# Graph and expert layers on one core: another order of VectorE's and TensorE's steps in the first node stage

## The chip, the core and the metric

The kernel runs on one core of a Trainium2 chip. A core has five engines that run their own instruction streams in order and wait for each other through semaphores: TensorE (PE, with its weight loads PEld), VectorE (DVE), ScalarE (ACT), GpSimd (POOL) and SyncE (SP), which issues most DMAs. The metric is the device time of one execution in microseconds (us), the median of the runs.

## The reference

Four layers follow each other on x, 10000 rows of 512 floats: a graph attention layer (8 heads of 64), an expert layer (8 experts, the best one of each row), a graph convolution and a second expert layer. The change is in the stage that ends the first layer and does the whole of the second for every row:

```
out = segment_sum(w[:, :, None] * x_l[src], dst)      # attention: own row and listed edges
x = x + elu(out + bias) + layernorm(x)
router_logits = xf @ Wr + br                          # xf = layernorm(x)
h  = relu(xf @ W1[e] + b1[e])                         # e = argmax(router_logits)
oe = h @ W2[e] + b2[e]
x = x + gate * oe                                     # one expert: the gate is 1
```

The stage also prepares the rows that the graph convolution gathers: the layernorm of the new x, scaled by a number a row.

## The kernel before

The rows lie in 79 tiles of 128 (NT = 79). The kernel is a row of stages with a barrier between two. The first node stage stands in lines 954 to 1385 of the profiled program; in it each engine goes through its own list of steps with `tiles_in_turn(NT, steps)`:

```
for t in range(n + max(lag for lag, _ in steps)):
    for lag, step in steps:
        if 0 <= t - lag < n:
            step(t - lag)
```

So in turn i of an engine a step with lag k works on tile i - k, and within a turn the steps run in the order in which the list names them. Nothing else orders the work of an engine; it can't pass a step whose semaphore is not there. The turns of different engines are tied by these semaphores alone. This is what is done for a tile, with the lag before, the tile written and the line:

- POOL: `edge_rows` gathers the tile's edge sums (ai, L1050); `average` (lag 3) adds ta and ts into oc (L1059); `minus_mean1` and `root1` make the numbers of the layernorm for two tiles at once (L1066, L1073, L1076).
- DVE: `listed_part` and `self_part` (lag 2) multiply edge sums and own row by their shares (ta L1183, ts L1190); `positive` (4) makes xq from oc and the residual (L1199); `negative` (5) makes x1 and its sum (L1211); `hidden` (11) takes the 264 columns of the up product out of PSUM, times the root, plus bias (hb, L1218); `best`, `its_number`, `number_f`, `one_hot` (11) find the expert (L1224 to L1241); `routed` (11) keeps the hidden values of that expert (hm, L1247); `add_experts` (14) adds the down product out of PSUM to x1 and gives x2 (L1260). Small steps once in four tiles (L1134 to L1167: softmax shares; L1268 to L1279: slopes and shifts) stand between.
- PE: `turn1` (8) transposes x1 (4 transposes, L154), `up` (9) multiplies it by wc (L148), `turn_h` (12) transposes hm (3 transposes, L154), `down` (13) multiplies by w2 and b2p (L1317, L1319).
- ACT: `exp_of` (4, mi, L1341), `spread1` (8, sum of squares, L1356), once in four tiles `exp_group` (L1331), `copy_h` (12) takes the transposed hidden values out of PSUM (hT and hTb, L1364 and L1365), `spread2` (19, L1373), `copy1` (8) takes the transposed x1 out of PSUM (x1T, L1347), `scaled` (25, gs, L1380).
- SP loads (L1026, L1029) and stores (L1033, L1037).

The waits that tie the turns of PE, ACT and DVE: `up(t)` waits for `copy1(t)` (c_x1T) and, since PSUM has two buffers, for `hidden(t - 2)` (c_hb); `copy1(t)` waits for `turn1(t)`; `copy_h(t)` waits for `turn_h(t)`; `down(t)` waits for `copy_h(t)` and `add_experts(t - 2)`; `turn_h(t)` waits for `routed(t)`; `add_experts(t)` waits for `down(t)` and `scaled(t - 12)`.

## Time and profile before

| | |
|---|---|
| median of 3 runs | 2910.95 us (2907.52 to 2920.2) |
| the profiled execution | 2923.28 us, its span 2921.6 us |
| first node stage | about 1069 to 1517 us of the span |
| PE, DVE, ACT, POOL busy over the whole span | 76%, 63%, 32%, 61% |
| granted TensorE clock, mean | 0.89 |

Busy time is the sum of an engine's instructions. The records of DVE and ACT overlap a little: the next one starts some 0.07 to 0.12 us before the last has ended, so what a step costs its engine is the distance from its start to the next one's start. A DVE record also grows when the instruction has to wait while it is on the engine, so a busy DVE may be a waiting one.

### The profile page before, as it was taken

The numbers are of one execution on the slowest core, as the hardware profiler recorded it, in microseconds if no ns is written. First come the engines' busy times: TensorE is split into PE (matmuls) and PEld (weight loads), VectorE is DVE, ScalarE is ACT, GpSimd is POOL, SyncE is SP. The second block draws the span as 40 slices with busy tenths as digits, with TensorE's granted clock in tenths as the row PEclk, the third lists the DMA queues.
The fourth block names the chain that finished last, engine by engine and source line by source line (L and its number), as shares of the span: only waits on it lengthen the run. The fifth ranks groups of instructions, "written<-read, shape, count | busy, mean of one in ns | idle before, by whom it ended". The sixth has DMA issues, their size and how long they took to land. (4 is left out here: it accounts for less than half of the span.)

```text
span 2921.6 us, 43538 instructions
## 1 busy us (share of the span) xinstructions
PE 2216.3 (76%) x11528; PEld 1300.0 (44%) x11554; DVE 1838.4 (63%) x5166; ACT 920.5 (32%) x2016; POOL 1786.6 (61%) x2143
## 2 busy tenths in 40 slices
PE   8999999847776737999978759999995677773000
PEld 3444444325554525666644326666663444442000
DVE  4776677524444449999941116777776567676666
ACT  1111111025444514777763315555553000000000
POOL 4555555566666437888736635777776555553776
PEclk9999999959999968999989979999997799997555
DMA  6655555467888746788749966667762899995999
GB/s 202 221 191 187 180 187 191 148 182 243 261 253 250 221 135 195 245 265 260 240 167 347 354 217 211 213 217 216 217 202 71 263 356 351 346 308 191 349 369 342
DMA packets 361396, 698.57 MB, mean 239 GB/s; under 512 B 51609, under 2 KB 85235, under 8 KB 361153
## 3 DMA queue, kind: packets, MB, share of 16 engines
q1 hardware_dynamic: 239672, 399.69, 40.1%
q0 software_dynamic: 76720, 217.93, 24.4%
q10 hardware_dynamic: 44761, 78.17, 7.4%
q8 instruction: 96, 1.57, 0.2%
q14 instruction: 147, 1.20, 0.1%
HBM read 426.08 MB, written 287.17 MB: 244 GB/s over the span
## 5 line engine op out<-in xcount | busy, mean ns | idle before, releaser
L2069 POOL DMA_INDIRECT xg<-n_rows,ids x219 | 219.0, 1000 | 168.3 <-PE psum L154 97.7
L148 PE MATMUL psum<-wl,xT 128*128 128x512 f32 x632 | 288.8, 600 | 0.0
L148 PE MATMUL psum<-wg,yT 128*128 128x512 f32 x632 | 286.1, 596 | 0.0
L148 PE MATMUL psum<-wr,xT 128*128 128x512 f32 x632 | 284.1, 592 | 0.0
L2219 POOL DMA_INDIRECT q<-slot_outputs,qs x158 | 173.9, 1101 | 86.2 <-issue 47.8
L337 ACT ACTIVATE xb<-xa,xsc 128x512 f32<-128x512 f32 x79 | 64.2, 814 | 480.4 <-POOL xsc L397 480.4
L1654 POOL DMA_INDIRECT slot_tokens<-sl x158 | 167.2, 1058 | 70.3 <-issue 65.6
L2157 DVE COPY gT<-psum 128x512 f32<-128x512 f32 x219 | 142.0, 685 | 107.8 <-PE psum L154 82.4
L154 PE MATMUL psum<-ident,xg 128*128 128x128 f32 x876 | 154.1, 307 | 71.6 <-issue 40.7
L384 POOL TENSOR_TENSOR ve<-mv,epst 128x1 f32<-128x1 f32 x79 | 51.1, 647 | 254.4 <-DVE mv L439 254.4
L684 POOL DMA_INDIRECT gl<-xl_rows,idx x118 | 129.3, 1096 | 117.6 <-DVE vv L736 68.2
L148 PEld LDWEIGHTS psum<-wr,xT 128*128 128x128 f32 x632 | 120.1, 190 | 151.2 <-issue 151.2
L148 PE MATMUL psum<-wc,x1T 128*128 128x264 f32 x632 | 162.1, 400 | 32.7 <-DVE hb L1218 25.1
L154 PEld LDWEIGHTS psum<-ident,xg 128*128 128x128 f32 x876 | 107.9, 155 | 157.6 <-issue 146.2
L1059 POOL TENSOR_TENSOR oc<-ta,ts 128x512 f32<-128x512 f32 x79 | 138.6, 1755 | 57.8 <-DVE ta L1183 28.8
L148 PEld LDWEIGHTS psum<-wl,xT 128*128 128x128 f32 x632 | 115.0, 190 | 120.2 <-issue 120.2
L148 PEld LDWEIGHTS psum<-wg,yT 128*128 128x128 f32 x632 | 114.7, 192 | 114.4 <-issue 114.4
L533 DVE SCALAR_TENSOR_TENSOR xl<-psum,rs,gb_b 128x512 f32<-128x512 f32 x79 | 59.2, 750 | 163.8 <-PE psum L148 163.8
L736 DVE TENSOR_TENSOR vv<-gl,wt 128x512 f32<-128x512 f32 x118 | 80.2, 682 | 122.8 <-issue 82.5
L1414 POOL DMA_INDIRECT gg<-gcn_rows,idx x118 | 118.2, 1002 | 62.3 <-issue 30.9
L688 POOL DMA_INDIRECT gr<-xr_rows,idx x118 | 126.6, 1073 | 42.1 <-issue 34.7
L148 PE MATMUL psum<-hp,x3T 128*128 128x256 f32 x632 | 149.9, 380 | 2.5 <-ACT x3T L2007 2.5
(316 smaller groups left out, 5453.6 us busy)
## 6 DMA issues: line engine op xcount, KB each, us to landing
slot_outputs<-yo ACTq DMA_DIRECT2D x54, 1024.0 KB
x_rows<-x SPq DMA_DIRECT2D x158, 256.0 KB
edge_sums<-eo SPq DMA_DIRECT2D x29, 1056.0 KB
edge_sums<-go SPq DMA_DIRECT2D x29, 1024.0 KB
xT<-in_xTt SPq DMA_DIRECT2D x79, 256.0 KB
xl_rows<-xl SPq DMA_DIRECT2D x79, 256.0 KB
xr_rows<-xr SPq DMA_DIRECT2D x79, 256.0 KB
residual_rows<-xb SPq DMA_DIRECT2D x79, 256.0 KB
```

The lines of the kernel that those rows point to most:

```text
L148: last = nc.tensor.matmul(ps, lhs[:, k, :], rhs[:, k, :], start=(k == 0), stop=(k == DK - 1))
L154: last = nc.tensor.transpose(ps[:, k * P:(k + 1) * P], rows[:, k * P:(k + 1) * P], ident[:])
L337: act.activation(xb[:, s, :], xa[:, s, :], ACT.Identity, scale=xsc[:, s, 1:2], bias=xsc[:, s, 0:1]).then_inc(a_xb, 1)
L684: pool.indirect_dma_start(gl[:, w % 16, :], None, XL, bass.IndirectOffsetOnAxis(idx[:, 0, w:w + 1], 0), bounds_check=NP - 1, oob_is_err=Fa ...
L688: pool.indirect_dma_start(gr[:, w % 8, :], None, XR, bass.IndirectOffsetOnAxis(idx[:, 1, w:w + 1], 0), bounds_check=NP - 1, oob_is_err=Fal ...
L736: nc.vector.tensor_tensor(heads(vv[:, w % 8, :], CE)[:, :, 0:C], heads(gl[:, w % 16, :]), wt[:, u % 2, j, :].unsqueeze(2).to_broadcast([P, ...
L1059: pool.tensor_tensor(oc[:, t % 3, :], ta[:, t % 3, :], ts[:, t % 3, :], ALU.add).then_inc(c_o, 1)
L1414: pool.indirect_dma_start(gg[:, w % 8, :], None, GR, bass.IndirectOffsetOnAxis(idx[:, 0, w:w + 1], 0), bounds_check=NP - 1, oob_is_err=Fal ...
L1654: pool.indirect_dma_start(IDXF, bass.IndirectOffsetOnAxis(sl3[:, k, t:t + 1], 0), sl3[:, 2, t:t + 1], None, bounds_check=ME * SLOTS * P - ...
L2069: pool.indirect_dma_start(xg[:, t % 8, :], None, XN3, bass.IndirectOffsetOnAxis(ids[:, t:t + 1], 0), bounds_check=NP - 1, oob_is_err=False ...
L2157: nc.vector.tensor_copy(gT[:, t % 8, :, :].rearrange("p k n -> p (k n)"), bank[t % 2]).then_inc(p_T, 1)
L2219: pool.indirect_dma_start(q0[:, b % 3, t % 4, k, :], None, YL, bass.IndirectOffsetOnAxis(qs[:, b % 3, t % 4, k:k + 1], 0), bounds_check=LI ...
```

## The change

Only the lists of steps are changed, none of the steps. POOL's `average` goes from lag 3 to 2, `minus_mean1` from 6 to 5. On DVE `listed_part` and `self_part` come first, then `hidden` and `add_experts`; `positive` (lag 4 to 3), `negative` (5 to 4) and `routed` come last; the steps on slopes and shifts go from lag 21 to 22. On PE `up` and `down` stand together and the two groups of transposes behind them. ACT's `exp_of` and `spread1` go one lag down.

```diff
-                tiles_in_turn(NT, ((3, average), (9, pairwise(root1)), (6, pairwise(minus_mean1)), (15, fourwise(minus_mean2)),
+                tiles_in_turn(NT, ((2, average), (9, pairwise(root1)), (5, pairwise(minus_mean1)), (15, fourwise(minus_mean2)),
...
-                    (11, hidden), (5, negative), (0, once(larger, 0)), (21, fourwise(slopes)), (11, best), (2, listed_part),
...
+                    (2, listed_part), (2, self_part), (11, hidden), (0, once(larger, 0)), (14, add_experts), (11, best),
...
-                tiles_in_turn(NT, ((8, turn1), (9, up), (12, turn_h), (13, down)))
+                tiles_in_turn(NT, ((9, up), (13, down), (8, turn1), (12, turn_h)))
...
-                tiles_in_turn(NT, ((4, exp_of), (8, spread1), (0, exp_group), (12, copy_h), (19, spread2), (8, copy1),
+                tiles_in_turn(NT, ((3, exp_of), (7, spread1), (0, exp_group), (12, copy_h), (19, spread2), (8, copy1),
```

One turn of PE in the middle of the stage, and the first step of the next, before:

```order
L148 MATMUL psum<-wc,x1T 128x264 x4
L154 MATMUL psum<-ident,hm 128x128 x3
L1317 MATMUL psum<-w,hT 128x512 x2
L1319 MATMUL psum<-b2p,hTb 128x512
L154 MATMUL psum<-ident,x 128x128 x4
L148 MATMUL psum<-wc,x1T 128x264 x4
```

The same in the changed program (line numbers are one less there):

```order
L148 MATMUL psum<-wc,x1T 128x264 x4
L1316 MATMUL psum<-w,hT 128x512 x2
L1318 MATMUL psum<-b2p,hTb 128x512
L154 MATMUL psum<-ident,x 128x128 x4
L154 MATMUL psum<-ident,hm 128x128 x3
L148 MATMUL psum<-wc,x1T 128x264 x4
```

The transposes of hm (`turn_h`) have moved from behind `up` to the end of the turn; between them and the next `up`, where the down products and the transposes of x1 stood, nothing is left.

ACT's stream of the changed program at the same place, from the copy that waits for `turn_h` on:

```order
L1363 ACTIVATE hT<-psum 128x256
L1364 ACTIVATE hTb<-psum 128x128
L1372 ACTIVATE sq,sB<-x2,sB 128x512
L1346 ACTIVATE x1T<-psum 128x512
L1379 ACTIVATE gs<-x2,sB 128x512
L1340 ACTIVATE mi<-oc 128x512
```

It is what it was: `copy_h`, `spread2`, `copy1`, `scaled`, `exp_of`; only the tiles of `exp_of` and `spread1` are later ones by one.

One turn of DVE without the small steps, before, from `hidden` on:

```order
L1218 SCALAR_TENSOR_TENSOR hb<-psum,sA,b1b 128x264
L1211 SCALAR_TENSOR_TENSOR x1,sA<-mi,xq 128x512
L1224 MAX m8<-hb 128x8
L1183 TENSOR_TENSOR ta<-ai,fe 128x512
L1229 MAX_INDEX i8<-m8,hb 128x8
L1190 TENSOR_TENSOR ts<-li,fe 128x512
L1234 CAST ix<-i8 128x1
L1199 SCALAR_TENSOR_TENSOR xq<-oc,xx 128x512
L1241 TENSOR_TENSOR hm<-iota3,ix 128x128
L1260 SCALAR_TENSOR_TENSOR x2,sB<-psum,x1 128x512
L1247 SCALAR_TENSOR_TENSOR hm<-hb,hm 128x256
```

And now, from `add_experts` on to the next `hidden`:

```order
L1260 SCALAR_TENSOR_TENSOR x2,sB<-psum,x1 128x512
L1224 MAX m8<-hb 128x8
L1229 MAX_INDEX i8<-m8,hb 128x8
L1234 CAST ix<-i8 128x1
L1241 TENSOR_TENSOR hm<-iota3,ix 128x128
L1199 SCALAR_TENSOR_TENSOR xq<-oc,xx 128x512
L1211 SCALAR_TENSOR_TENSOR x1,sA<-mi,xq 128x512
L1247 SCALAR_TENSOR_TENSOR hm<-hb,hm 128x256
L1183 TENSOR_TENSOR ta<-ai,fe 128x512
L1190 TENSOR_TENSOR ts<-li,fe 128x512
L1218 SCALAR_TENSOR_TENSOR hb<-psum,sA,b1b 128x264
```

The two products that POOL's sum waits for now stand directly ahead of the two steps that read PSUM, and `routed` (hm<-hb,hm) stands as far from the start of that sum as it can.

## Rows read from the trace of the kernel before

**Rows 1.** The page: its engines' busy time, and DVE in 40 slices.
```profile
PE 2216.3 (76%) x11528; PEld 1300.0 (44%) x11554; DVE 1838.4 (63%) x5166; ACT 920.5 (32%) x2016; POOL 1786.6 (61%) x2143
...
DVE  4776677524444449999941116777776567676666
```

**Rows 2.** Busy time by stretch: PE, PEld, DVE, ACT, POOL, clock, DMA share, GB/s.
```profile
1150.00:1425.00 275.00, 257.73 (x1082) 168.89 (x1098) 274.90 (x902) 197.72 (x497) 224.66 (x230) 1.00 0.80 253
```

**Rows 3.** Groups of DVE, 1150 to 1425: count, busy us, mean ns, idle before.
```profile
L1247 DVE SCALAR_TENSOR_TENSOR hm<-hb,hm 128x256 f32<-128x256 f32 x55 | 48.2, 877 | 0.0
...
L1162 DVE RECIPROCAL rd<-rd 128x32 f32<-128x32 f32 x13 | 4.4, 342 | 0.0
```

**Rows 4.** Instructions on the tile hb, whole trace: min/median/max ns.
```profile
L1247 DVE SCALAR_TENSOR_TENSOR hm<-hb,hm x79: 413/883/1374, 1118.3 to 1499.9; 128x256 f32<-128x256 f32 x79
```

**Rows 5.** Timeline of POOL and DVE: start, duration, engine, line, tiles.
```profile
1311.87 1.72 POOL L1059 TENSOR_TENSOR oc<-ta,ts 128x512 f32<-128x512 f32 x1
...
1312.37 0.68 DVE L1260 SCALAR_TENSOR_TENSOR x<-psum,x 128x512 f32<-128x512 f32 x1
...
1312.98 0.88 DVE L1247 SCALAR_TENSOR_TENSOR hm<-hb,hm 128x256 f32<-128x256 f32 x1
```

**Rows 6.** Waits, 1100 to 1500: who waited for whom, us, times, longest.
```profile
ACT hT L1364 <- PE psum L154: 92.6, 70, 2.8
...
PE psum L148 <- DVE hb L1218: 25.1, 49, 2.9
```

**Rows 7.** Timeline of PE: the start of a turn, and the next turn.
```profile
1309.71 2.02 PE L148 MATMUL psum<-wc,x1T 128*128 128x264 f32 x8 [0.33 <-DVE hb L1218]
...
1314.41 2.02 PE L148 MATMUL psum<-wc,x1T 128*128 128x264 f32 x8
1316.27 0.49 PE L154 MATMUL psum<-ident,hm 128*128 128x128 f32 x3
1316.60 1.88 PE L1317 MATMUL psum<-w,hT 128*128 128x512 f32 x4
1318.32 0.38 PE L1319 MATMUL psum<-b2p,hTb 128*128 128x512 bf16 x1
1318.53 0.60 PE L154 MATMUL psum<-ident,x 128*128 128x128 f32 x4
```

**Rows 8.** Timeline of ACT, the same turn.
```profile
1316.80 0.38 ACT L1364 ACTIVATE hT<-psum 128x256 f32<-128x256 f32 x1 [1.04 <-issue]
...
1317.94 0.59 ACT L1347 ACTIVATE x1T<-psum 128x512 f32<-128x512 f32 x1
1318.42 0.82 ACT L1380 ACTIVATE gs<-x,sB 128x512 f32<-128x512 f32 x1
1319.12 0.63 ACT L1341 ACTIVATE mi<-oc 128x512 f32<-128x512 f32 x1
```

**Rows 9.** Timeline, how soon PE follows on a copy it waited for.
```profile
1105.43 0.58 ACT L1347 ACTIVATE x1T<-psum 128x512 f32<-128x512 f32 x1
...
1106.06 0.81 PE L148 MATMUL psum<-wc,x1T 128*128 128x264 f32 x1 [7.54 <-ACT x1T L1347]
```

**Rows 10.** Timeline of PE, `up` of tile 3 and of tile 78 (merged rows).
```profile
1120.20 2.66 PE L148 MATMUL psum<-wc,x1T 128*128 128x264 f32 x7 [2.91 <-DVE hb L1218]
...
1492.11 1.16 PE L148 MATMUL psum<-wc,x1T 128*128 128x264 f32 x4
```

**Rows 11.** Timeline near the stage's end, where DVE waits for ACT.
```profile
1488.37 0.69 DVE L1260 SCALAR_TENSOR_TENSOR x<-psum,x 128x512 f32<-128x512 f32 x1 [1.98 <-ACT gs L1380]
```

**Rows 12.** Busy time by stretch (columns as rows 2), for the clock.
```profile
700.00:900.00 200.00, 146.32 (x1395) 106.15 (x1393) 93.65 (x177) 97.23 (x233) 124.63 (x114) 0.92 0.84 256
1600.00:1690.00 90.00, 73.08 (x244) 34.63 (x243) 9.67 (x15) 34.52 (x61) 61.48 (x62) 1.00 0.99 355
...
1113.00:1117.00 4.00, 2.21 (x12) 1.88 (x12) 4.00 (x11) 2.33 (x6) 3.81 (x4) 1.00 0.57 188
1120.00:1125.00 5.00, 4.46 (x15) 3.49 (x15) 4.96 (x17) 1.28 (x5) 3.93 (x5) 0.66 0.54 165
```

More of the change, by code:

```diff
@@ L1281, in _ @@
                 tiles_in_turn(NT, (
-                    (11, hidden), (5, negative), (0, once(larger, 0)), (21, fourwise(slopes)), (11, best), (2, listed_part),
-                    (0, once(below, 0)), (21, fourwise(shifts)), (11, its_number), (2, self_part),
-                    (0, once(edge_share, 1)), (21, fourwise(shifts_up)), (11, number_f), (4, positive),
-                    (0, once(weight_sum, 1)), (11, one_hot), (0, once(inverse, 1)), (14, add_experts), (11, routed),
-                    (0, once(shares, 1))))
+                    (2, listed_part), (2, self_part), (11, hidden), (0, once(larger, 0)), (14, add_experts), (11, best),
+                    (0, once(below, 0)), (22, fourwise(slopes)), (11, its_number), (0, once(edge_share, 1)),
+                    (22, fourwise(shifts)), (11, number_f), (22, fourwise(shifts_up)), (11, one_hot), (3, positive),
+                    (0, once(weight_sum, 1)), (4, negative), (0, once(inverse, 1)), (11, routed), (0, once(shares, 1))))
             @block.tensor
```

## The prediction

> **What bounds the kernel now.** I read the page first. Its slices show one stretch where VectorE is at nine tenths or more, slices 16 to 20, and that stretch is the stage which the change touches [rows 1]. The busy time by stretch then says how hard VectorE is bound there: 274.90 of 275 us, with TensorE at 257.73 and its clock at 1.00 throughout, POOL at 224.66, ACT at 197.72 [rows 2]. The next question is what fills VectorE. The groups show `routed` (L1247) at 877 ns a tile [rows 3], although its shortest record is 413 [rows 4]; a 256 column step should not cost more than the 512 column ones. The timeline says why: it starts at 1312.98 while POOL's sum has been running since 1311.87, the sum ends at 1313.59, and `routed` ends 0.27 us later, at 1313.86 [rows 5]. So `routed` stands still until the sum is over, about 0.46 us a tile (877 - 413). The waits say who else suffers: TensorE waited 25.1 us in all for `hidden` [rows 6].
>
> The second engine is close behind. Its turn that starts at 1314.41 had to wait for nothing: it came 4.70 us behind the start of the one before, 1309.71 [rows 7]. The waits' largest line, ACT's `copy_h` for TensorE, 92.6 us [rows 6], reads like nothing, as ACT has time to spare. It is the line on which this forecast rests: ACT comes early to the step that waits for `turn_h`, and all that stands behind it on ACT waits too.
>
> **The period before.** `up` of tile 3 starts at 1120.20, `up` of tile 78 at 1492.11 [rows 10]: 371.9 us for 75 turns, 4.96 us each.
>
> **VectorE's new order, and POOL's sum a tile sooner.** No instruction is added or taken away. The two products now stand ahead of `hidden` and `add_experts`, so the sum (L1059) starts right behind the second product. Of the steps that fall beside it, those out of PSUM do not stand still: `add_experts` at 1312.37 took its usual 0.68 us in the middle of a sum [rows 5]. `routed` comes late in the turn. The gain is at most 877 - 413 = 0.46 us a tile, so VectorE would need 4.96 - 0.46 = 4.50 us a turn. At worst the wait only moves to `one_hot` or `positive` and the gain is nothing. I take the full 0.46, and it is worth nothing on the path, because the next part makes a slower loop.
>
> The Trainium skill has a rule for what rows 5 show (SBUF — State Buffer, section on the two separate sides): VectorE instructions with two SBUF inputs and GpSimd instructions share one pair of ports, which goes to whoever starts first, for its whole instruction. The trace agrees, with `routed` ending 0.27 us behind the sum. By that rule alone the change would be a gain, and that is the third rival below.
>
> **TensorE's new order.** Before, a turn was x1 transposes, up, hm transposes, down. Now it is up, down, x1 transposes, hm transposes. The step to follow is the next `up`. It needs x1T, which ACT's `copy1` makes of the x1 transposes of the turn just ended. ACT's order is not changed: `copy_h`, `spread2`, `copy1`. And `copy_h` waits for the hm transposes, now TensorE's last work in the turn. As ACT can't pass a waiting step, `copy1` cannot run while TensorE is still at its turn, although its own input would be there; and TensorE cannot go on before `copy1` is through. This closes a loop of one turn:
>
> - up to down: 1316.27 - 1314.41 = 1.86 us [rows 7];
> - w2 products: 1318.32 - 1316.60 = 1.72; b2p product: 1318.53 - 1318.32 = 0.21 [rows 7];
> - four transposes of x1: three take 1316.60 - 1316.27 = 0.33, so 0.11 each and 0.44 for four [rows 7];
> - three transposes of hm until ACT starts on them: 1316.80 - 1316.27 = 0.53 [rows 7, 8];
> - ACT from the start of `copy_h` over `spread2` to the end of `copy1`: 1317.94 + 0.59 - 1316.80 = 1.73 [rows 8];
> - TensorE's start behind `copy1`: 1106.06 - (1105.43 + 0.58) = 0.05 [rows 9], and since that row may show the weight load rather than the product, up to 0.15; I take 0.10.
>
> The sum is 1.86 + 1.72 + 0.21 + 0.44 + 0.53 + 1.73 + 0.10 = 6.59 us a turn. Before, `down` and the x1 transposes (1.72 + 0.21 + 0.58 = 2.51 us) stood between `turn_h` and the next `up`, and hid the 1.73 us of ACT. That cover is gone. Fewer changes between products and transposes could give some of the switching time back: a wait-free turn before was 4.70, while my pieces up to the last transpose give 4.76 with 0.20 of it drain; so at most 0.1 us. Bounds: 6.45 to 6.75.
>
> Times 75 turns (turn 12, where `turn_h` first comes, to turn 86, the last with a `copy1`): 75 x 6.59 = 494, against 371.9 before: **+122 us** (+112 to +134 by the bounds). Turns ahead and behind have no such loop. Their end is ACT's run of `spread2` and `scaled`, which is as long as it was.
>
> **Does another engine make the loop longer?** `add_experts` waits for `scaled` of ACT's turn before, a wait that before had near the end of the stage, 1.98 us [rows 11]. From the start of `add_experts` to the end of the next `hidden` VectorE has one whole turn of work, 4.50 us with the small steps at their mean; seven of those fall in one turn of four, the longest of them 0.34 [rows 3], for which I allow 1.0 more. Then come 0.10 + 4.76 on TensorE, 1.73 on ACT, 0.70 for `scaled` (1318.42 to 1319.12) [rows 8] and 0.10 to the next `add_experts`: 11.9 us, at most 12.9. This loop spans two turns, so 5.9 to 6.4 a turn, less than 6.59. POOL's work of a turn was 224.66 of 275 us with its waits for ports, 4.1 us, and fits. SP's queue is moved past nothing. The slopes a turn later delay `scaled`, which is waited for late in the turn; no cost.
>
> **The clock.** TensorE now stands still 1.83 us (1.73 + 0.10) in each turn of 6.59, so it is busy 72%. Rows at either end: from 1600 to 1690 it was busy 81% at clock 1.00, and in 1113 to 1117, with a hole of 1.8 us, at 1.00 too; in the edge stage, busy 73%, the mean was 0.92, and from 1120 to 1125, behind a hole of 2.91 us, 0.66 [rows 10, 12]. A mean of 0.92 between the levels of 2.4 and 1.2 GHz is 16% of the time at the lower, where TensorE's 72% runs at half speed: 0.16 x 0.72 x 0.5 = 5.8% of 494, or 28 us. So 0 to 28; the hole here is nearer to the first kind, the busy share to the second, and I take the middle, **+14 us**.
>
> **Sum.** The profiled execution: 2923.3 + 122 + 14 = 3059 us. It was 12.3 us above the median of the runs, so the median becomes 2911 + 136 = 3047 us.
>
> **The rivals.**
>
> *The clock falls for good* (slower still). Holes come in every turn here, which no stretch of before shows. At a mean of 0.75, half of the time at the lower level, the loop grows by 0.5 x 0.72 x 0.5 = 18%, 89 us instead of 14: 3122 us. For it: the drop behind 2.91 us [rows 12]. Against: the hole is 1.8, and such holes kept 1.00.
>
> *VectorE's loop binds after all.* If the small steps, or a stand-still behind POOL's sum, make 5.9 to 6.4 into 7.0, the stage gains another 75 x 0.4 = 30 us: 3077 us. For it: VectorE is tightly packed, and `hidden` now waits behind both products. Against: the margin of 0.2 at worst, and VectorE has some 2 us free in each turn.
>
> *Faster* (the other side). If ACT's chain is not in the way, TensorE's 4.70 to 4.76 bounds the turn, since VectorE needs only 4.50: 75 x (4.96 - 4.76) = 15 us, to 2896 us. It decides at the hm transposes: `copy1` would have to end within 0.1 us of them. For it: the 0.46 us of `routed` is real. Against: the order of ACT's stream, in which `copy1` stands behind `copy_h`. It would need my reading of one wait to be wrong.
>
> *The change does nothing that counts*: the loop is partly covered and eats only what VectorE wins, 2911 us. Same objection.
>
> **How the numbers follow.** About 0.5% (15 us) is what a measurement of this kernel can tell from no change. Forecast 0.80, clock 0.07, VectorE's loop 0.06, faster 0.04, nothing 0.03. The forecast's own range is +112 to +134 and 0 to 28 for the clock: 3023 to 3073; with the second rival it reaches to 3085, which is wide enough for 8 in 10. Slower by over 0.5%: 0.93. The case of 2896 lies on the bound, so it is split: faster 0.03, within 0.5% 0.04.
>
> **What would show it.** In the profile of the changed kernel `up` starts some 6.6 us apart, and the waits have a new first line for TensorE: L148 for ACT's x1T, some 1.8 us in each turn, 130 us or more, where now it is 25.1 us for hb. `routed` falls to about 415 ns. VectorE's idle time moves to `add_experts`, waiting for gs, some 1.5 to 2 us a turn. The prediction is wrong if L148 doesn't wait for x1T, if the period stays under 5 us, or if the clock column of the stage falls under 0.85.

## The result and the profile after

The changed kernel takes 3034.97 us (median of 4 runs, 3027.68 to 3039.05) where the kernel before takes 2909.23 us (median of 4, 2905.54 to 2920.2). The ratio is 1.0426, with a 95% interval from 1.0402 to 1.0450: slower by 125.7 us. The forecast was 3047 us with a range from 3023 to 3085.

The profiled execution took 3027.68 us, its span 3026.0. Here is the page's busy time by engine and VectorE in 40 slices, to be read beside [rows 1]:

```profile
PE 2208.4 (73%) x11528; PEld 1300.6 (43%) x11554; DVE 1849.8 (61%) x5166; ACT 919.5 (30%) x2016; POOL 1724.8 (57%) x2143
...
DVE  5776676434444487777762112777777477677665
```

The instruction counts are the same and the busy times nearly so, but the nines of VectorE in the stage have become sevens. The busy time of the middle of the stage says the same more sharply (columns as in [rows 2]: PE, PEld, DVE, ACT, POOL, clock, DMA share, GB/s):

```profile
1150.00:1550.00 400.00, 288.87 (x1207) 190.91 (x1225) 310.63 (x1000) 218.44 (x552) 191.31 (x251) 1.00 0.60 190
```

No engine is full now: VectorE 78%, TensorE 72%, ACT 55%, POOL 48%, with the clock at 1.00. Something that is not the work of one engine sets the time. The waits of the stage, 1100 to 1620, name it (who waited for whom: us in total, times, longest):

```profile
ACT hT L1363 <- PE psum L154: 232.2, 78, 4.1
...
PE psum L148 <- ACT x1T L1346: 145.3, 76, 13.6
...
PE psum L148 <- DVE hb L1218: 5.5, 2, 3.1
```

TensorE's wait for `hidden`, 25.1 us in [rows 6], is down to 5.5, and in its place `up` waits for ACT's x1T 76 times (once for 13.6 us at the start of the stage, then for about 1.8 us in a turn). One turn in the timeline of PE and ACT, from one `up` to the next (start, duration, engine, line, tiles, and the wait before it), is the loop itself:

```profile
1354.85 2.05 PE L148 MATMUL psum<-wc,x1T 128*128 128x264 f32 x8 [1.83 <-ACT x1T L1346]
...
1356.73 1.88 PE L1316 MATMUL psum<-w,hT 128*128 128x512 f32 x4
1358.67 0.60 PE L154 MATMUL psum<-ident,x 128*128 128x128 f32 x4
...
1359.10 0.49 PE L154 MATMUL psum<-ident,hm 128*128 128x128 f32 x3
1359.63 0.38 ACT L1363 ACTIVATE hT<-psum 128x256 f32<-128x256 f32 x1 [2.92 <-PE psum L154]
...
1360.07 0.72 ACT L1372 ACTIVATE sq<-x,sB 128x512 f32<-128x512 f32 x1
...
1360.77 0.59 ACT L1346 ACTIVATE x1T<-psum 128x512 f32<-128x512 f32 x1
...
1361.42 1.82 PE L148 MATMUL psum<-wc,x1T 128*128 128x264 f32 x7 [1.82 <-ACT x1T L1346]
```

The x1 transposes are through by 1359.27. `copy1`, which needs only them, starts at 1360.77, because `copy_h` (L1363) stands ahead of it on ACT and waits until 1359.63 for the hm transposes, and `spread2` stands between the two. `up` follows 0.06 us behind `copy1`'s end, 1361.42 - 1361.36. From `up` to `up` it is 6.57 us.

What the forecast said of `routed` came about too. These are its records on the tile hb (min/median/max ns), as in [rows 4], and then the groups of POOL's sum and of `add_experts` from 1200 to 1500, as in [rows 3]:

```profile
L1247 DVE SCALAR_TENSOR_TENSOR hm<-hb,hm x79: 360/420/427, 1115.0 to 1615.8; 128x256 f32<-128x256 f32 x79
```

```profile
L1059 POOL TENSOR_TENSOR oc<-ta,ts 128x512 f32<-128x512 f32 x46 | 57.9, 1259 | 141.3 <-DVE ta L1183 141.3
L1260 DVE SCALAR_TENSOR_TENSOR x<-psum,x 128x512 f32<-128x512 f32 x45 | 31.1, 692 | 62.5 <-issue 58.0 <-ACT gs L1379 4.5
...
L1134 DVE TENSOR_TENSOR mxn<-ai,selfa 128x32 f32<-128x32 f32 x11 | 12.5, 1134 | 0.0
```

`routed` went from a median of 883 ns to 420, and the sum from a mean of 1769 ns (before, 1150 to 1425) to 1259: neither stands in the other's way now. VectorE's free time lies at `add_experts`, 62.5 us in 45 turns. The profile puts only 4.5 us of it down to ACT's gs, but in the turn above `scaled` runs from 1354.68 to 1355.50 and `add_experts` starts at 1355.59, right behind it. And the last of these rows is a first sign of something that the forecast did not have: a step on 32 columns, `larger`, that takes 1134 ns.

**Where the time went in the stage.** I take the stage from the cast of b2p (L1109) to the first gather of the next stage: 1069.2 to 1522.1 = 452.9 us before, 1062.7 to 1639.2 = 576.5 after, a difference of 123.6. It splits at the same two places as [rows 10]:

| part of the stage | before | after | difference |
|---|---|---|---|
| to `up` of tile 3 (1120.20; 1117.16) | 51.0 | 54.5 | +3.5 |
| 75 turns to `up` of tile 78 (1492.11; 1604.55) | 371.9 | 487.4 | +115.5 |
| behind it | 30.0 | 34.6 | +4.6 |

The two profiled spans differ by 104.4 us only, less than the stage and less than the medians. Outside the stage no step is changed; it is the medians and their ratio that measure the change.

### The profile page after: what moved, and what is told of

Same layout as the page of the kernel before. It is cut to its first block and busy times, and to the rows that moved or that the text cites. A ratio compares the mean times of both kernels' runs of the same rounds, so it can differ in the third digit from the quotient of the medians.

```text
span 3026.0 us, 43538 instructions
## 1 busy us (share of the span) xinstructions
PE 2208.4 (73%) x11528; PEld 1300.6 (43%) x11554; DVE 1849.8 (61%) x5166; ACT 919.5 (30%) x2016; POOL 1724.8 (57%) x2143
## 5 line engine op out<-in xcount | busy, mean ns | idle before, releaser
L148 PE MATMUL psum<-wc,x1T 128*128 128x264 f32 x632 | 164.9, 405 | 152.0 <-ACT x1T L1346 145.3
L1059 POOL TENSOR_TENSOR oc<-ta,ts 128x512 f32<-128x512 f32 x79 | 101.6, 1286 | 213.1 <-DVE ta L1183 188.1
L148 PEld LDWEIGHTS psum<-wc,x1T 128*128 128x128 f32 x632 | 115.6, 193 | 187.4 <-ACT x1T L1346 163.8
L154 PE MATMUL psum<-ident,xg 128*128 128x128 f32 x876 | 145.0, 300 | 56.7 <-issue 30.8
L2163 DVE COPY yo<-psum 128x512 f32<-128x512 f32 x219 | 136.5, 683 | 31.6 <-PE psum L2099 17.2
```

The costliest lines, as they stand in the source:

```text
L148: last = nc.tensor.matmul(ps, lhs[:, k, :], rhs[:, k, :], start=(k == 0), stop=(k == DK - 1))
L154: last = nc.tensor.transpose(ps[:, k * P:(k + 1) * P], rows[:, k * P:(k + 1) * P], ident[:])
L1059: pool.tensor_tensor(oc[:, t % 3, :], ta[:, t % 3, :], ts[:, t % 3, :], ALU.add).then_inc(c_o, 1)
L2163: nc.vector.tensor_copy(yo[:, t % 12, :], bank[4 + t % 4]).then_inc(p_y, 1)
```

## The experiments

Every kernel here computes the whole of the reference; only orders and lags differ. The kernel before ran beside each series, and it took 2892.16 us in that of E1 to E4, 2907.86 in that of E5 and E7 to E9, 2789.10 in that of E11 and E12, and 2787.16 in that of E13 and E14, each series on a chip of its own. So ratios within a series are compared, not times across them. For a finer look there is the distance from one `larger` (L1134, once in four turns) to the next, in the steady middle of the stage. There is one trace of the kernel before, and the stage and the turns of every run are compared with it. That is fair across the series, since in all twelve runs the difference of the stage from 452.9 us agrees with the difference of the medians within 5.2 us. The runs go by the numbers of their labels (there is no 6 and no 10) and are told in the order of the questions.

| kernel | ratio, 95% interval | whole stage, us | four turns, us |
|---|---|---|---|
| before | 1 | 452.9 | 20.08 |
| after | 1.0426 (1.0402 to 1.0450) | 576.5 | 26.3 |
| E2: PE's new order alone | 1.0440 (1.0405 to 1.0474) | 575.8 | 26.3 |
| E1: after, with PE's old order | 1.0080 (1.0056 to 1.0105) | 475.7 | 21.24 |
| E4: after, hm transposes first | 1.0335 (1.0301 to 1.0370) | 547.1 | 24.66 |
| E5: after, `scaled` inside the loop | 1.0642 (1.0614 to 1.0671) | 648.7 | 30.8 |
| E3: after, `copy1` ahead of `copy_h` | 1.0391 (1.0349 to 1.0434) | 559.3 | 24.4, later up to 27.8 |
| E9: E1 with `larger` and `below` moved | 1.0049 (1.0033 to 1.0066) | 465.0 | 20.64 |
| E8: before, the sum sooner alone | 1.0173 (1.0145 to 1.0201) | 502.0 | 22.75 |
| E12: E8 with POOL's root first | 1.0046 (1.0030 to 1.0061) | 469.2 | 21.3 |
| E7: mixed order | 1.0478 (1.0451 to 1.0506) | 592.3 | 28.0 |
| E11: spaced order | 1.0048 (1.0031 to 1.0065) | 466.3 | 20.83 |
| E13: before, `routed` behind `negative` | 0.9980 (0.9967 to 0.9992) | 446.3 | 19.75 |
| E14: before, `routed` behind `hidden` | 0.9971 (0.9958 to 0.9984) | 444.5 | 19.75 |

### E2 and E1: is it PE's order, and it alone?

E2 is the kernel before with PE's new list and nothing else. E1 is the changed kernel with PE's old list.

```diff
 E2, to the kernel before
-                tiles_in_turn(NT, ((8, turn1), (9, up), (12, turn_h), (13, down)))
+                tiles_in_turn(NT, ((9, up), (13, down), (8, turn1), (12, turn_h)))
 E1, to the changed kernel
-                tiles_in_turn(NT, ((9, up), (13, down), (8, turn1), (12, turn_h)))
+                tiles_in_turn(NT, ((8, turn1), (9, up), (12, turn_h), (13, down)))
```

> The kernel before with nothing but TensorE's list in the new order (up, down, turn1, turn_h). Theory L: turns of 6.57 us (5.88 in the seven turns without spread2), as in the changed kernel, so 3025 to 3040 us, and TensorE waits some 1.8 us a turn for x1T. Rival V: near the time before, 2905 to 2920 us.

> The changed kernel with TensorE's list of steps as before (turn1, up, turn_h, down); the new orders of VectorE, POOL and ACT stay. Theory L (a loop of one turn: the hm transposes, ACT's copy_h, spread2 and copy1, the next up): down and the x1 transposes cover ACT again, TensorE's own 4.70 to 4.76 us a turn bounds the stage, 75 x (4.96 - 4.75) = 16 us less than before: 2893 us (2885 to 2911), routed at some 415 ns. Rival V (VectorE's new order makes the stage slow, because hidden and add_experts now come behind both products and POOL is pinned to them): stays near the changed kernel's 3035 us, turns of about 6.5 us.

E2: 3018.95 against 2892.16 us, ratio 1.0440. The intervals of E2 and of the whole change overlap almost wholly: the one line gives the whole slowdown. Its timeline of PE has the same period and the same hole:

```profile
1351.82 2.05 PE L148 MATMUL psum<-wc,x1T 128*128 128x264 f32 x8 [1.83 <-ACT x1T L1347]
...
1358.39 2.05 PE L148 MATMUL psum<-wc,x1T 128*128 128x264 f32 x8 [1.83 <-ACT x1T L1347]
```

It runs at 6.57 us with VectorE's old order, so VectorE's new order has no part in the period. E2 also shows that the fall of `routed` in the changed kernel proves nothing for that order: in E2's longer turn, with the old one, its median is 421 ns too. That the loop goes away without PE's list is E1's half: there `up` does not wait for x1T any more, and the kernel is back at 2916.68 against 2892.16.

But E1 is not faster than before, as VectorE's share of the change should have made it (the forecast for E1 was 16 us less; the new lags of POOL and ACT are in it too). It is 0.8% slower, although `routed` takes 404 ns. The groups of E1 from 1150 to 1450:

```profile
L1260 DVE SCALAR_TENSOR_TENSOR x<-psum,x 128x512 f32<-128x512 f32 x56 | 38.2, 682 | 4.2 <-ACT gs L1379 4.2
L1247 DVE SCALAR_TENSOR_TENSOR hm<-hb,hm 128x256 f32<-128x256 f32 x57 | 23.1, 404 | 0.0
L1134 DVE TENSOR_TENSOR mxn<-ai,selfa 128x32 f32<-128x32 f32 x14 | 16.2, 1156 | 0.0
```

and the same `larger` in the kernel before, 1150 to 1425:

```profile
L1134 DVE TENSOR_TENSOR mxn<-ai,selfa 128x32 f32<-128x32 f32 x14 | 2.5, 181 | 0.0
```

The timeline of DVE and POOL in E1 shows two causes side by side. First the turn with `larger`:

```profile
1306.92 1.27 POOL L1059 TENSOR_TENSOR oc<-ta,ts 128x512 f32<-128x512 f32 x1 [0.71 <-DVE ta L1183]
1307.11 1.14 DVE L1134 TENSOR_TENSOR mxn<-ai,selfa 128x32 f32<-128x32 f32 x1
```

`larger` reads two operands out of SBUF, starts 0.19 us behind the sum and ends 0.06 us behind the sum's end: 1156 - 181 = 0.97 us lost, once in four turns. The sum did not lose its victim; it found another. A second small one is `slopes` (L1268, also once in four turns), 425 ns on average here and 195 before. The Trainium skill's rule (SBUF — State Buffer, section on the two separate sides), that whoever starts first keeps the shared ports for its whole instruction, fits this too: here the price goes by what is left of the sum, not by the size of the step that is caught.

The second cause shows best in a turn without `larger`:

```profile
1297.83 0.17 DVE L1224 MAX8 m<-hb 128x8 f32<-128x8 f32 x1
...
1298.11 0.16 DVE L1229 FIND_INDEX8 i<-m,hb 128x8 uint32<-128x8 f32 x1
1298.30 0.15 DVE L1234 CAST ix<-i 128x1 f32<-128x1 uint32 x1
1298.56 0.29 DVE L1241 TENSOR_TENSOR hm<-iota,ix 128x128 f32<-128x128 f32 x1
1298.77 0.69 DVE L1199 SCALAR_TENSOR_TENSOR xq<-oc,xx 128x512 f32<-128x512 f32 x1
```

`best`, `its_number`, `number_f` and `one_hot` each need the result of the one before. Back to back they hold VectorE for 1298.77 - 1297.83 = 0.94 us. In the kernel before they stand between large steps, and from each start to the next start on the engine they take 0.08 + 0.15 + 0.06 + 0.20 = 0.49 us there. In E1 they take 0.94 and 0.97 us in the two turns of four in which nothing stands between them, 0.81 in the one with `below` behind `best`, and 0.55 in the one with a small step behind each (from 1292.30). So it is standing right behind the one they need that costs, 0.33 us a turn on average, two thirds of what `routed` had won.

The sum over four turns: `routed` 4 x (0.404 - 0.877) = -1.89, the four small steps 0.94 + 0.97 + 0.81 + 0.55 - 4 x 0.49 = +1.31, `larger` +0.97, `slopes` +0.23, `add_experts` waiting for gs 4.2 / 56 x 4 = +0.30. Together +0.92, and measured are 21.24 - 20.08 = +1.16; what the last 0.24 is made of was not followed up. So VectorE's new order, meant to relieve it, costs it 0.29 us a turn.

### E4 and E5: is the loop what the sum says it is?

If the loop is right in its parts, then another order of its members must change the period by a computed amount. E4 puts the hm transposes ahead of the x1 transposes, so that `copy_h` no longer waits for the last work of the turn. E5 puts `scaled` between `spread2` and `copy1`, and so into the loop.

```diff
 E4, PE
-                tiles_in_turn(NT, ((9, up), (13, down), (8, turn1), (12, turn_h)))
+                tiles_in_turn(NT, ((9, up), (13, down), (12, turn_h), (8, turn1)))
 E5, ACT
-                tiles_in_turn(NT, ((3, exp_of), (7, spread1), (0, exp_group), (12, copy_h), (19, spread2), (8, copy1),
-                                   (25, scaled)))
+                tiles_in_turn(NT, ((3, exp_of), (7, spread1), (0, exp_group), (12, copy_h), (19, spread2), (25, scaled),
+                                   (8, copy1)))
```

> The changed kernel with the hm transposes ahead of the x1 transposes on TensorE (up, down, turn_h, turn1). Theory L: the chain on ACT starts 0.44 us earlier, under the four x1 transposes, so turns of 6.13 us: 3035 - 75 x 0.44 = 3002 us. If instead copy1 itself waits for the x1 transposes that now come last, so that their place at the end decides, nothing is gained: 3035 us.

> The changed kernel with ACT's scaled ahead of copy1, so that its 0.70 us lies in the loop from the hm transposes to the next up. Theory L: turns of 6.57 + 0.70 = 7.27 us from turn 25 on, 62 of them, 43 us more than the changed kernel, which was 1.0426 of the kernel before: about 168 us above the kernel before. TensorE's hole becomes 2.53 us a turn. If such a hole, coming in every turn, lowers the granted clock, turns grow beyond 7.5 us and the whole beyond 190 us above before; if the hole of every turn is harmless at any size near this one, the clock of the stage stays at 1.00.

E4: 2989.03 against 2892.16 us, ratio 1.0335. `up` starts every 6.13 us, except once in four turns, when it waits for `hidden` instead and the turn is about 6.29 us. In the others it has a hole of 1.39 instead of 1.83, shorter by the 0.44 us of the four transposes that now lie beside ACT's copies:

```profile
1350.79 2.05 PE L148 MATMUL psum<-wc,x1T 128*128 128x264 f32 x8 [1.39 <-ACT x1T L1346]
...
1356.92 2.05 PE L148 MATMUL psum<-wc,x1T 128*128 128x264 f32 x8 [1.39 <-ACT x1T L1346]
```

E5: 3098.60 against 2907.86 us, ratio 1.0642. The hole is now 2.53 us, longer by 0.70, as long as `scaled` holds ACT (1318.42 to 1319.12 in [rows 8]), and the period is 7.27 us, or 8.96 (1353.15 to 1362.11) in every third or fourth turn:

```profile
1353.15 2.83 PE L148 MATMUL psum<-wc,x1T 128*128 128x264 f32 x8 [2.53 <-ACT x1T L1346]
...
1362.11 2.05 PE L148 MATMUL psum<-wc,x1T 128*128 128x264 f32 x8 [2.53 <-ACT x1T L1346]
...
1369.39 2.05 PE L148 MATMUL psum<-wc,x1T 128*128 128x264 f32 x8 [2.53 <-ACT x1T L1346]
```

In both, the turns that the loop alone sets fit it to 0.01 us. E5 as a whole takes 190.7 us more than the kernel before, where 168 was forecast for the loop alone. The rest is what the changed kernel has not, TensorE's lower clock. The busy time of four microseconds in the turn of 8.96 us (the number behind POOL's is the clock):

```profile
1352.00:1356.00 4.00, 2.85 (x9) 2.29 (x10) 3.30 (x17) 2.32 (x5) 0.47 (x1) 0.78 0.50 137
```

In the turn from 1353.15 `up` takes 2.83 us instead of 2.05. Every third or fourth turn is such a one, and loses 8.96 - 7.27 = 1.69 us.

### E3: is `copy1` behind `copy_h` all that is wrong?

The loop closes because ACT's `copy1` can't pass `copy_h`. E3 puts it ahead.

```diff
-                tiles_in_turn(NT, ((3, exp_of), (7, spread1), (0, exp_group), (12, copy_h), (19, spread2), (8, copy1),
-                                   (25, scaled)))
+                tiles_in_turn(NT, ((3, exp_of), (7, spread1), (0, exp_group), (8, copy1), (12, copy_h), (19, spread2),
+                                   (25, scaled)))
```

> The changed kernel with ACT's copy1 ahead of copy_h and spread2; TensorE's new order stays. Theory L: copy1 (0.59 us) now runs while TensorE does the hm transposes; from up to the x1 transposes 3.79 us, from their start to the next up about 1.3 us, so turns of 5.1 us: 2911 + 75 x 0.14 = 2921 us (2905 to 2935). Rival T (it is TensorE's own order that costs, products apart from transposes, whatever ACT does): stays near 3035 us.

3003.71 against 2892.16 us, ratio 1.0391: nearly as slow as the changed kernel, and a clear miss. It is not rival T, though, in which TensorE's own order costs: for the first dozen turns, and again for the last few, the period is 5.1 us, as computed. From 1183.70 on, longer and shorter turns follow each other, and `up` waits for `hidden` in each:

```profile
1189.25 2.02 PE L148 MATMUL psum<-wc,x1T 128*128 128x264 f32 x8 [0.83 <-DVE hb L1218]
...
1195.61 2.02 PE L148 MATMUL psum<-wc,x1T 128*128 128x264 f32 x8 [1.64 <-DVE hb L1218]
...
1201.49 2.02 PE L148 MATMUL psum<-wc,x1T 128*128 128x264 f32 x8 [1.17 <-DVE hb L1218]
```

```profile
1183.70:1268.00 84.30, 66.02 (x280) 43.70 (x280) 71.10 (x233) 50.41 (x128) 47.89 (x60) 1.00 0.67 218
```

Two turns take 11.9 to 12.5 us there (1201.49 - 1189.25 = 12.24), with the clock at 1.00. From 1274.69 on it gets worse. The timeline of a later pair:

```profile
1397.81 2.95 PE L148 MATMUL psum<-wc,x1T 128*128 128x264 f32 x8 [1.96 <-DVE hb L1218]
...
1400.55 2.69 PE L1316 MATMUL psum<-w,hT 128*128 128x512 f32 x4
...
1404.57 2.05 PE L148 MATMUL psum<-wc,x1T 128*128 128x264 f32 x8 [0.36 <-ACT x1T L1346]
...
1406.45 0.69 DVE L1260 SCALAR_TENSOR_TENSOR x<-psum,x 128x512 f32<-128x512 f32 x1 [3.53 <-ACT gs L1379]
...
1411.39 0.91 PE L148 MATMUL psum<-wc,x1T 128*128 128x264 f32 x3 [2.07 <-DVE hb L1218]
```

`add_experts` (L1260) waits 3.53 us for `scaled`, and behind it on VectorE stands the next `hidden`, for which `up` then waits: this is the loop over two turns that the forecast had as a rival. The holes are 1.9 to 3.0 us now in nearly every second turn, and behind most of these the clock falls for a few microseconds, 0.59 from 1398 to 1402:

```profile
1398.00:1402.00 4.00, 4.00 (x10) 2.67 (x10) 3.75 (x13) 1.21 (x3) 3.65 (x6) 0.59 0.37 113
```

The two turns shown take 1411.39 - 1397.81 = 13.58 us. `up` and `down` at the lower clock lose (2.95 - 2.05) + (2.69 - 1.88) = 1.71 of it, which leads back to the 11.9 us that such a pair took while the clock was at 1.00. The forecast's working for that loop was 11.9 to 12.9. So the changed kernel had two loops of nearly the same length, 6.57 us and some 6 a turn, and taking away the longer one could give little.

### E9: how much of VectorE's loss is `larger`?

E1 again, with `larger` and `below` ahead of the products.

```diff
-                    (2, listed_part), (2, self_part), (11, hidden), (0, once(larger, 0)), (14, add_experts), (11, best),
-                    (0, once(below, 0)), (22, fourwise(slopes)), (11, its_number), (0, once(edge_share, 1)),
+                    (0, once(larger, 0)), (2, listed_part), (0, once(below, 0)), (2, self_part), (11, hidden), (14, add_experts),
+                    (11, best), (22, fourwise(slopes)), (11, its_number), (0, once(edge_share, 1)),
```

> The changed kernel with TensorE's old list (as in e1, which took 24 us more than before) and with larger and below, the two small softmax steps, ahead of the products instead of behind hidden and best. In e1 larger (L1134) takes 1.06 us instead of 0.18 because it meets POOL's sum. If that is one of the two losses of VectorE's new order, 19 turns with 0.9 us less: 17 us less than e1, about 7 us above before. If the stand-still only moves to the next step with two SBUF inputs, as in e1.

2923.34 against 2907.86 us, ratio 1.0049, where E1 has 1.0080. `larger` takes 178 ns again:

```profile
L1260 DVE SCALAR_TENSOR_TENSOR x<-psum,x 128x512 f32<-128x512 f32 x59 | 40.3, 683 | 8.6 <-ACT gs L1379 8.6
...
L1134 DVE TENSOR_TENSOR mxn<-ai,selfa 128x32 f32<-128x32 f32 (+1 forms) x15 | 2.7, 178 | 0.0
```

Against the kernel before that is 15.5 us, where E1 had 24.5 and the forecast was 7. Four turns are 20.64 instead of 21.24: 0.60 won of the 0.97. The waits of `add_experts` for gs have doubled, 8.6 us in 59 turns against 4.2 in 56, which is 0.28 in four turns and takes most of the rest back. The order as a whole stays slower than before.

### E8 and E12: what does the sum a turn sooner do by itself?

E8 is the kernel before with `average` at lag 2. E12 also puts POOL's `root1` ahead of it.

```diff
 E8
-                tiles_in_turn(NT, ((3, average), (9, pairwise(root1)), (6, pairwise(minus_mean1)), (15, fourwise(minus_mean2)),
+                tiles_in_turn(NT, ((2, average), (9, pairwise(root1)), (6, pairwise(minus_mean1)), (15, fourwise(minus_mean2)),
 E12
+                tiles_in_turn(NT, ((9, pairwise(root1)), (2, average), (6, pairwise(minus_mean1)), (15, fourwise(minus_mean2)),
```

> The kernel before with POOL's average at lag 2 instead of 3 and nothing else. If routed's stand-still of 0.46 us a tile comes from where the sum falls, an earlier sum moves it to another step with two SBUF inputs (positive or one_hot) without removing it: same as before within 0.5%. If the sooner sum alone is what helps, VectorE's turn falls from 5.02 to about 4.7 us and the kernel is 20 us faster.

> As e8 (the kernel before with POOL's average at lag 2), with POOL's root1 ahead of average in its list. e8 took 1.7% more than before, and its hidden waited 25.5 us in 300 for the root that POOL makes behind the sum. If root1 standing behind a sum that waits for VectorE's self_part is the cause, its time comes back to before within 0.5%. If the sum's new place beside other VectorE steps is the cause, it stays over 1% slower.

E8: 2961.19 against 2907.86 us, ratio 1.0173, worse than either theory had it. The timeline of E8 shows a wait that was not there before:

```profile
1301.74 1.94 POOL L1059 TENSOR_TENSOR oc<-ta,ts 128x512 f32<-128x512 f32 x1 [0.74 <-issue]
...
1304.09 0.71 POOL L1076 TENSOR_TENSOR sA<-sA,mhalf 128x2 f32<-128x2 f32 x1
...
1304.92 0.49 DVE L1218 SCALAR_TENSOR_TENSOR hb<-psum,sA,b1b 128x264 f32<-128x264 f32 x1 [0.96 <-POOL sA L1076]
```

`hidden` needs the root that POOL makes for two tiles at once, and the root now stands behind a sum that starts late in the turn, when the second product is through. `up`, which waits for `hidden`, has a hole of 2.53 us in this turn. The waits of 1150 to 1450 have it 26 times:

```profile
DVE hb L1218 <- POOL sA L1076: 25.5, 26, 1.3
```

E12 takes the root from behind the sum, and the ratio falls to 1.0046: about three quarters of the loss was this wait. Most of the rest is another wait that the sooner sum brings. `slopes`, once in four turns, now comes before POOL has its numbers ready (E12, 1100 to 1400):

```profile
DVE sB L1268 <- POOL sB L1094: 10.7, 13, 0.8
```

That is 0.8 us of the 1.2 that four turns take more. The whole change moves the slopes to lag 22 and puts the products at the head of VectorE's turn, and in the middle of the stage neither the changed kernel nor E1 has this wait or that of `hidden` for the root.

### E7 and E11: a version of my own

Both keep PE's and ACT's old order, or nearly so, and spread VectorE's small steps between the large ones, with those out of PSUM beside the sum. The core of E7, and of E11, in VectorE's list:

```diff
 E7, with average at lag 2
+                    (11, hidden), (14, add_experts), (11, best), (4, positive), (11, its_number), (0, once(larger, 0)),
+                    (21, fourwise(slopes)), (5, negative), (11, number_f), (0, once(below, 0)), (21, fourwise(shifts)),
+                    (0, once(edge_share, 1)), (11, one_hot), (21, fourwise(shifts_up)), (0, once(weight_sum, 1)),
+                    (2, listed_part), (0, once(inverse, 1)), (11, routed), (0, once(shares, 1)), (2, self_part)))
 E11, with root1 ahead of average at lag 2, and ACT's scaled ahead of copy1, spread2 behind it
+                    (0, once(larger, 0)), (2, listed_part), (12, routed), (0, once(below, 0)), (2, self_part), (11, hidden),
+                    (14, add_experts), (11, best), (3, positive), (11, its_number), (21, fourwise(slopes)),
+                    (0, once(edge_share, 1)), (4, negative), (11, number_f), (21, fourwise(shifts)),
+                    (0, once(weight_sum, 1)), (11, one_hot), (0, once(inverse, 1)), (21, fourwise(shifts_up)),
```

> The kernel before (TensorE, ACT and all lags but one unchanged) with POOL's average at lag 2 and VectorE's turn in an order of my own: hidden and add_experts behind self_part, the four steps that find the expert apart from each other with large steps between, small steps late. If both losses of the changed order (stand-still of small steps beside the sum, steps that wait for the one just ahead) and the stand-still of routed are avoided, VectorE needs about 4.5 us and TensorE's 4.70 bounds the turn: 75 x 0.25 = 15 to 19 us less than before. If they only move, within 0.5% of before.

> A version of my own: TensorE's list of before; VectorE's products first, hidden and add_experts behind them beside the sum, the steps that find the expert apart from each other, routed behind the next turn's first product; POOL's root1 ahead of the sum; ACT's scaled ahead of copy1 and spread2 behind it, so that add_experts finds it done. If the losses read from e1 and e9 (small steps beside the sum, steps waiting for the one just ahead, add_experts waiting for scaled) are all there is, VectorE needs 4.7 us a turn, as TensorE does, and the kernel takes 12 to 19 us less than before. If they only move, within 0.5% of before.

E7: 3047.83 against 2907.86 us, ratio 1.0478, a bad miss, and for E8's reason. With `self_part` last and `hidden` first, the root waits behind the sum and `hidden` behind the root (waits of 1150 to 1450):

```profile
PE psum L148 <- DVE hb L1218: 66.3, 21, 4.7
DVE hb L1218 <- POOL sA L1076: 57.6, 22, 2.9
```

The holes reach 4.7 us, and the clock of 1150 to 1450 is 0.87.

E11: 2802.34 against 2789.10 us, ratio 1.0048, where 12 to 19 us less was hoped for. It has none of the waits named so far: `routed` 421 ns, `larger` 192, `add_experts` without idle time. And yet four turns take 20.83, 0.75 more than before, and VectorE is busy for 98% of the time from 1100 to 1350. The group of `positive` in that stretch says why:

```profile
L1199 DVE SCALAR_TENSOR_TENSOR xq<-oc,xx 128x512 f32<-128x512 f32 x48 | 54.8, 1143 | 0.0
```

It took 676 ns in the kernel before. Here it stands behind `hidden`, `add_experts` and `best`, and in the turn from 1200.58 it starts at 1201.67, while the sum runs from 1200.80 to 1202.08. On average it pays 0.47 us a turn, as much as `routed` wins: the sum has found a large step again.

### E13 and E14: only `routed` moved

The least change that still takes `routed` away from the sum: in the kernel before, `routed` goes to the next turn (lag 12), behind `negative` (E13) or between `hidden` and `negative` (E14). Nothing else is touched.

```diff
 E13
-                    (11, hidden), (5, negative), (0, once(larger, 0)), (21, fourwise(slopes)), (11, best), (2, listed_part),
+                    (11, hidden), (5, negative), (12, routed), (0, once(larger, 0)), (21, fourwise(slopes)), (11, best), (2, listed_part),
 E14
+                    (11, hidden), (12, routed), (5, negative), (0, once(larger, 0)), (21, fourwise(slopes)), (11, best), (2, listed_part),
```

> The kernel before with one step moved: routed (lag 12 instead of 11, so one turn later) stands behind hidden and negative instead of behind add_experts. In before it stands still 0.46 us a tile behind POOL's sum. Behind add_experts now comes hidden, which reads PSUM and need not wait, so only some 0.1 us of the sum is left when negative comes: VectorE's turn falls from 5.02 to about 4.7 us, TensorE's 4.70 us bounds, and the kernel takes 15 to 24 us less than before. If the stand-still only moves to negative, or TensorE's hm transposes now wait for routed, within 0.5% of before.

> As e13, but routed stands between hidden and negative, 0.6 us sooner. routed then may still meet the last 0.1 to 0.2 us of the sum, and TensorE's hm transposes find it sooner. If the stand-still is what costs, as fast as e13 or up to 10 us slower, and faster than before; if TensorE waits for hm in e13, this one is faster than e13.

E13: 2782.61 against 2787.16 us, ratio 0.9980 (0.9967 to 0.9992). E14: 2777.77, ratio 0.9971 (0.9958 to 0.9984). Both are faster than the kernel before by more than their intervals, and both by a fraction of the 0.46 us a turn: 4.6 and 9.4 us, where E13 was to give 15 to 24 unless the stand-still moved. The groups of 1100 to 1350 say why, E13 first:

```profile
L1211 DVE SCALAR_TENSOR_TENSOR x<-mi,xq 128x512 f32<-128x512 f32 x51 | 50.7, 993 | 0.0
L1247 DVE SCALAR_TENSOR_TENSOR hm<-hb,hm 128x256 f32<-128x256 f32 x51 | 21.1, 414 | 0.0
```

and E14:

```profile
L1247 DVE SCALAR_TENSOR_TENSOR hm<-hb,hm 128x256 f32<-128x256 f32 x51 | 34.2, 671 | 0.0
```

In E13 `routed` is at its full 414 ns, 0.46 less than in the kernel before, but `negative`, the step that now reaches the sum's end, grew from 675 to 993. In E14 `negative` takes 680, and it is `routed` again that is caught, for 671 instead of 877. Once in four turns the step that is caught begins 0.11 us ahead of the sum by the records (in E14 `routed` at 1252.74, the sum at 1252.85) and still stands still for the whole of it, 1.69 us; which of two starts as close as that was first can't be read from them. Small steps beside the sum pay too: `shares` (L1167) takes 403 and 445 ns in the two, 212 before. Four turns are 19.75 in both, 0.33 less than before. E13 and E14 are the fastest versions found; their intervals overlap, so which of the two is the faster is not shown.

## Why the prediction was right, and where it was not

**The loop (right).** The step that decided was to read ACT's large wait for the hm transposes [rows 6] not as idle time that costs nothing but as a place where everything behind it on ACT is held. E2 gives the whole loss with the one line; E4 and E5 move the period by the computed 0.44 and 0.70 us. The pieces from [rows 7 to 9] gave 6.59 us a turn and 6.57 was measured; one by one they were off by 0.04 us at most (TensorE's start behind `copy1`, 0.06 where I took 0.10).

**How many turns (slightly off).** I took the full 6.59 for all 75 turns. In the first seven of them ACT has no `spread2` yet, and they take 5.88 us six times and 5.30 once: 6 x 0.69 + 1.27 = 5.4 us less. The 0.02 in each of the other turns makes 1.5. So the term was +115.5 instead of +122.

**Head and tail (missed, small).** "Their end is ACT's run of `spread2` and `scaled`, which is as long as it was", and the slopes a turn later at no cost: together the two ends took 3.5 + 4.6 = 8.1 us more. That it made up for the seven turns is luck. How much of it is the slopes' later turn was not tested.

**The clock (mis-sized).** I took +14 us as the middle of 0 and 28; it was 0. The clock was 1.00 from 1150 to 1550. Of the two rows that I stood between, the one with a hole of 1.8 us at clock 1.00 was the right one and the busy share of 73% the wrong one: TensorE was busy 72% here too. E5 and E3 show that the danger was near: with holes of 2.53 us the clock fell in every third or fourth turn, and in E3 it fell behind one of 1.92. The rival of 3122 us, a mean clock of 0.75, did not come even there: E5 has 0.95 from 1150 to 1450. Without this term the forecast would have been 3033 us, and 3035 was measured; the last 2 us rest on the luck just named. The step from the profiled execution to the median was a weak one as well: I put it at -12.3 us, but the profiled execution of the changed kernel, forecast at 3059, took 3027.68, which is 7.3 us below its median.

**VectorE's new order (wrong, without effect).** I took the gain as the full 0.46 us a turn, with "nothing" as the worst case. E1 shows a loss of 0.29 (with the lags of POOL and ACT), outside of that range. I had looked for the sum's next victim among the large steps only, and not at `larger`, and I took the dependent small steps at their mean from an order in which they stood apart. On the path it counted for nothing, since the loop hid it, but it means that the rival of 2896 us was priced wrong as well: had the loop not been there, the change would have come out as E1 does, 0.8% slower and not 0.5% faster.

**VectorE's two-turn loop (right in size, near).** 5.9 to 6.4 us a turn was my working; in E3, where it binds, a turn takes 5.9 to 6.3 with the clock at 1.00. Its pieces were not all right: in two turns of E3 VectorE took 4.84 and 5.41 us from the start of `add_experts` to the end of the next `hidden` (4.50 to 5.50 in my working), TensorE 4.43 to the start of `copy1` (4.76; the hm transposes come behind `copy1` there) and ACT 2.43 from there to the end of `scaled` (1.73 + 0.70). With 4.76 in place of 4.43, as TensorE's order in the changed kernel has it, the same pieces make an estimated 6.1 to 6.4 a turn. It was right that it does not bind at 6.57, but the margin is 0.2 to 0.4 us.

**What would show it.** Of the signs that I named, these came: `up` 6.57 us apart, 145.3 us of waiting for x1T, `routed` at 420 ns, the stage's clock not under 0.85. VectorE is idle at `add_experts`, as named, but for 62.5 / 45 = 1.4 us a turn, a little less than the 1.5 to 2.

## What to carry to other kernels

When steps on one engine are reordered, follow what the last step of the turn releases: if the next turn's first step needs something that another engine, working in order, can give only behind that release, the chain of both is a loop, and its sum is the period, whatever the busy shares say. A large wait on an engine with time to spare is harmless only as long as nothing behind it is urgent. And a stall behind another engine's instruction is not removed by moving its victim: look at what stands in that place then, the smallest step included, and at what dependent small steps cost once they stand next to each other.

## What the runs showed of the hardware that I had not expected

- **The price of a stall goes by what is left of POOL's sum, not by the size of the step that stalls.** In E1 `larger`, 181 ns by itself on 32 columns, started 0.19 us behind the sum's start and took 1.14 us. In the kernel before `routed`, 413 ns on 256 columns, started 1.11 us behind it and took 0.88. `add_experts`, out of PSUM, took its usual 0.68 us at 1297.23 of E1, inside a sum from 1297.05 to 1298.31.
- **Dependent small steps cost about twice as much back to back**, 0.94 us for four against 0.49 spread among large ones, and 0.55 with one small step behind each (E1, from 1292.30).
- **Regular holes and TensorE's clock.** A hole of 1.83 us in each turn of 6.57 left the clock at 1.00 (2.4 GHz) for 400 us on end; a hole of 2.53 in each turn of 7.27 lost it in every third or fourth turn, in which `up` took 2.83 us instead of 2.05, and the turn 1.69 us longer. In E3 the clock stayed at 1.00 from 1183.70 to 1268.00 with unequal holes of 0.54 to 1.95 us, and then fell behind one of 1.92 (`up` at 1274.69 took 2.71 us). So the size of the last hole alone does not decide it; what does was not tested.
- **The same kernel differs between chips by more than most changes here.** The median of the kernel before was 2787 to 2909 us, 4% apart, in series on different chips, while its runs within a series lie within 0.6%. The stage studied here has no visible part in it. In the traces of E11 to E14 it begins at 984 to 993 us, in all others at 1060 to 1069, so some 70 to 80 us of the difference lie ahead of it. Whether it is the chip or something else that differed between the series was not tested.
